# Turning the adapter activations in TensorE's transposing mode in a four-layer LoRA chain

## The chip, the cores and the metric

The kernel runs on one core of a Trainium2 chip. The metric is the device time of one execution in microseconds (us), as a median over several executions; lower is better. One more execution was recorded by the hardware profiler, and everything said of engines and waits below comes from that one.

## The reference, cut to what matters

Four residual layers are applied one after the other to `x` (8 batches of 256 tokens, 1024 features, fp32):

```python
x = x + L0(x)   # base weight quantized to a codebook, plus a LoRA of rank 64
x = x + L1(x)   # base weight, plus 8 experts of rank 16, top 2 by a softmax gate per token
x = x + L2(x)   # base weight and bias, plus the batch's own adapter of rank 16
x = x + L3(x)   # one of 16 weights, chosen by batch
```

The part that the change touches is in L2:

```python
lora_h = jnp.einsum('bti,bir->btr', x, A)         # 16 numbers per token: "h2"
lora_out = jnp.einsum('btr,bro->bto', lora_h, Bm)
return base_out + lora_out * SCALING
```

`lora_h` comes out of the kernel's products with tokens on the partitions, and the second product needs it with its rank on the partitions. So it has to be turned.

## The kernel before

**Phase 1** (about the first 230 us) multiplies the weights of L0, L1 and L2 into one another, so that the first three layers become a few wide products of `x`. Nearly every product is one of fp32 values, each split into a rounded high part and a remainder (type fp32r), in three matmuls: high by high, high by low, low by high (`product`, lines 992 to 994).

**Phase 2** runs over four groups `g` of 512 tokens (two batches each), three of them in a loop on every engine and the last written out. On TensorE a group is, in this order (`group`, written by hand):

- `x3_main(g, m)`: the m-th of eight blocks of 128 output features, 24 matmuls of 512 columns into bank `m % 5` of PSUM. `x3_main(g, 0)` comes first.
- `low_rank(g)`: for each of four tiles of 128 tokens, the expert activations, the gate's logits and h2, into banks 4 to 7 (lines 1079 and 1081). ScalarE and VectorE bring them to SBUF as `tok`; ScalarE then copies the h2 columns into `h2_tok`, 128 tokens by 32 columns per tile (16 for each batch, the other batch's columns zero), and VectorE works out the gates (`gating`) and scales the expert columns of `tok` by them.
- `x3_main(g, 1)`, `x3_main(g, 2)`.
- `turn_h2(g)` (lines 1116 to 1121): four matmuls with `h2_tok` as weights and the identity as moving operand put the turned h2 into partitions 0 to 31 of bank 5. `h2_tok` lies in the memory of `scales`, so the profile calls these `ps<-ident,scales`.
- `turn_g(g)` (lines 1123 to 1129): four 128 by 128 `pe.transpose` of the gated expert columns into bank 7. The profile calls these `ps<-ident,e_mid_w`.
- `x3_main(g, 3)`, then `h2_add(g)`, which adds onto bank 5 what the experts contribute to h2. It waits for `gt_done`: ScalarE (line 683) and VectorE (line 731) have brought bank 7 to SBUF.
- `x3_main(g, 4)`, then the gate and closing products of each block. `x3_close` needs the finished h2 (`h2_done`).
- `y_product(g, 0)` and `y_product(g, 1)`: L3, 192 matmuls of 512 columns each with weights streamed from HBM by SyncE's queue, split by ScalarE and VectorE into rings of four half tiles.

`turn_h2` raises no semaphore of its own. Its result is read after `h2_add`, whose last matmul raises `h2t_mm`.

Of the kernel before, what the change touches and what calls it, by code (L numbers as in the profile page):

```python
# [118 lines left out]
def build(nc, x, cb, lang, id2, id3, w0, scale_log, lora_a, lora_bt, w1, wrt, at, bcat,  # L119
          w2t, b, las, lbs, w3t, y):  # L120
    plan = phase1_plan()
    with ExitStack() as ctx:
# [866 lines left out]
        def _(pe):  # L989
# [126 lines left out]
            def turn_h2(g):  # L1116

                pe.wait_ge(h2_tok_done, 2 * (g + 1))
                for t in range(4):
                    pe.matmul(ps[0:32, 5, t * P:(t + 1) * P], h2_tok[:, t, :], ident[:, :],  # L1120
                              start=t == 0, stop=False, skip_group_check=True)

            def turn_g(g):

# [35 lines left out]
            def group(g):  # L1160
                x3_main(g, 0)
                low_rank(g)
                x3_main(g, 1)
                x3_main(g, 2)
                turn_h2(g)
                turn_g(g)
                x3_main(g, 3)
                h2_add(g)
                x3_main(g, 4)
                for m in range(3):  # L1170
                    x3_gate(g, m)
                pe.wait_ge(h2_done, g + 1)
                pe.wait_ge(bs_done, BS_CREDIT + 2 * (g + 1))
                for m in range(3):
                    x3_close(g, m)
                for m in range(3, 5):
                    x3_gate(g, m)
                    x3_close(g, m)
                for m in range(5, KT):
                    x3_main(g, m)  # L1180
                    x3_gate(g, m)
                    x3_close(g, m)
                y_product(g, 0)
                y_product(g, 1)
# [44 lines left out]
```

## Time and profile before

| | before |
|---|---|
| median of 3 runs | 678.62 us (678.43 to 678.86) |
| the profiled execution's own time | 679.95 us |
| its span (first to last instruction) | 678.1 us |
| TensorE matmuls, busy | 664.5 us, 98% of the span, 3280 instructions |
| TensorE weight loads, busy | 569.2 us, 84% |
| VectorE busy | 353.8 us, 52% |
| ScalarE busy | 279.3 us, 41% |
| GpSimd busy | 86.5 us, 13% |
| DMA | 67.59 MB, mean 100 GB/s |

A matmul of the program stands in the trace as a weight load (PEld) and a matmul (PE). Matmuls are pipelined: the duration of one, for example 273 ns, reaches over the start of the next, so what a matmul takes of TensorE's time is the distance from its start to the next one's start. The granted TensorE clock is given in tenths or as a number up to 1.00.

### The profile page before, as it was taken

To read this page: it belongs to the slowest core of one execution; us is meant where nothing else is said; L and a number is where in the kernel's file an instruction comes from. 1 tells how busy PE (TensorE), PEld (TensorE's weight loads), DVE (VectorE), ACT (ScalarE), POOL (GpSimd) and SP (SyncE) were. 2 spreads that over 40 slices of the span, in tenths; PEclk is the share of its full clock that TensorE was granted. 3 is DMA by queue.
4 is the path that set the end of the run, shared out by engine and by line. 5 is a ranking of instruction groups with operands and counts; after the bars stand their busy time and mean duration, and the time that the engine had idled before them with its cause. 6 is when DMAs were issued, how large, how long until landed. Compare 5 with 4: busy or idle time off the path is not lost.

```text
span 678.1 us, 9248 instructions
## 1 busy us (share of the span) xinstructions
PE 664.5 (98%) x3280; PEld 569.2 (84%) x3280; DVE 353.8 (52%) x535; ACT 279.3 (41%) x418; POOL 86.5 (13%) x122
## 2 busy tenths in 40 slices
PE   5998999999999999999999999999999999999998
PEld 5898999999999988888888788888788888888886
DVE  5689989879971384024543222661421653412453
ACT  5557483971912371124552122562121564121353
POOL 3210115004010030000120000221000221000120
PEclk9999999999999999999999999999999999999999
DMA  9661312001000504002774000677000586000362
GB/s 317 171 200 31 94 32 63 1 0 63 1 0 1 187 12 137 1 0 94 280 239 156 0 0 31 245 249 240 0 0 0 186 281 210 28 1 1 96 230 108
DMA packets 39330, 67.59 MB, mean 100 GB/s; under 512 B 3588, under 2 KB 23044, under 8 KB 39300
## 3 DMA queue, kind: packets, MB, share of 16 engines
q1 hardware_dynamic: 34448, 59.07, 26.7%
q10 hardware_dynamic: 4852, 8.13, 3.4%
q8 instruction: 18, 0.29, 0.2%
q14 instruction: 12, 0.10, 0.1%
HBM read 58.80 MB, written 8.39 MB: 99 GB/s over the span
## 4 chain that ended last, share of the span: by engine, by line
PE 92%; SPq 4%; DVE 2%; ACT 1%; issue 1%; DMA 0%; POOL 0%; ACTq 0%; DVEq 0%; POOLq 0%
PE ps L992 28%; PE ps L994 28%; PE ps L993 28%; PE ps L1079 3%; PE ps L1081 1%; SPq L342 1%; SPq L367 1%; PE ps L1112 1%; DVE tmp L802 1%; PE ps L1120 1%; SPq L366 1%; ACT tmp L547 0%; DMA e_both_w<-w_t 0%; SPq L337 0%; DVE w_w L792 0%
## 5 line engine op out<-in xcount | busy, mean ns | idle before, releaser
L992 PE MATMUL ps<-e_both,ring_hi 128*128 128x384 f32 (+3 forms) x384 | 134.6, 351 | 10.2 <-DVE e_both L731 8.3
L731 DVE TENSOR_TENSOR ring_lo<-raw,ring_hi 128x512 fp32r<-128x512 f32 x128 | 92.5, 736 | 80.9 <-ACT ring_hi L643 80.7
L994 PE MATMUL ps<-e_both,ring_lo 128*128 128x384 f32 (+3 forms) x384 | 134.1, 349 | 0.0
L643 ACT ACTIVATE ring_hi<-raw 128x512 fp32r<-128x512 f32 x128 | 79.4, 629 | 70.1 <-PE ps L994 65.9
L992 PE MATMUL ps<-x_both,e_both 128*128 128x512 f32 x256 | 101.5, 396 | 0.0
L993 PE MATMUL ps<-x_both,e_both 128*128 128x512 f32 x256 | 101.2, 395 | 0.0
L994 PE MATMUL ps<-x_both,e_both 128*128 128x512 f32 x256 | 101.0, 395 | 0.0
L992 PE MATMUL ps<-ring_hi,e_mid 128*128 128x512 f32 x256 | 101.0, 395 | 0.0
L994 PE MATMUL ps<-ring_hi,e_mid 128*128 128x512 f32 x256 | 101.0, 395 | 0.0
L993 PE MATMUL ps<-ring_lo,e_mid 128*128 128x512 f32 x256 | 101.0, 394 | 0.0
L992 PEld LDWEIGHTS ps<-e_both,ring_hi 128*128 128x128 f32 x384 | 72.8, 190 | 15.8 <-DVE e_both L731 8.3
L493 POOL TENSOR_TENSOR raw<-raw,ident 128x128 f32<-128x128 f32 x64 | 40.4, 633 | 320.2 <-DMA raw<-w_t 320.2
L994 PEld LDWEIGHTS ps<-e_both,ring_lo 128*128 128x128 f32 x384 | 72.7, 189 | 5.7
L966 DVE SCALAR_TENSOR_TENSOR e_mid<-ps,bias_col,e_mid 128x512 fp32r<-128x512 f32 x32 | 22.6, 746 | 94.7 <-ACT e_mid L689 94.7
L993 PE MATMUL ps<-e_mid,ring_hi 128*128 128x384 f32 (+2 forms) x192 | 68.5, 357 | 0.0
L993 PE MATMUL ps<-e_both,ring_hi 128*128 128x384 f32 (+2 forms) x192 | 65.5, 341 | 0.0
L547 ACT ACTIVATE tmp<-tmp,dif 128x1024 f32<-128x1024 f32 x48 | 54.1, 1150 | 21.3 <-DVE tmp L800 18.2
L802 DVE SCALAR_TENSOR_TENSOR tmp<-w_w,thr,tmp 128x1024 f32<-128x1024 f32 x48 | 60.4, 1302 | 4.4 <-ACT tmp L547 4.1
L689 ACT ACTIVATE e_mid<-ps,bias_col 128x512 fp32r<-128x512 f32 x32 | 20.4, 687 | 96.6 <-PE ps L1112 96.6
L993 PEld LDWEIGHTS ps<-ring_lo,e_mid 128*128 128x128 f32 x256 | 48.2, 188 | 11.3
L994 PEld LDWEIGHTS ps<-ring_hi,e_mid 128*128 128x128 f32 x256 | 48.2, 188 | 11.3
L994 PEld LDWEIGHTS ps<-x_both,e_both 128*128 128x128 f32 x256 | 48.1, 188 | 11.4
(144 smaller groups left out, 855.5 us busy)
## 6 DMA issues: line engine op xcount, KB each, us to landing
raw<-w_t SPq DMA_DIRECT2D x64, 512.0 KB, 3.6
xraw<-x_t SPq DMA_DIRECT2D x16, 512.0 KB, 4.8
w_w<-w SPq DMA_DIRECT2D x15, 512.0 KB, 5.1
y<-tmp ACTq DMA_DIRECT2D x30, 256.0 KB, 2.9
e_both_w<-w_t SPq DMA_DIRECT2D x4, 512.0 KB, 8.8
e_both_w<-w_t SPq DMA_DIRECT2D x4, 384.0 KB, 6.0
e_mid_w<-bs SPq DMA_DIRECT2D x24, 64.0 KB, 2.8
e_mid_w<-b_cat SPq DMA_DIRECT2D x1, 512.0 KB, 7.1
```

The source lines that it names most:

```text
L342: sp.dma_start(e_lo_w[:, ks, cols], w2t[2 * kk * P:2 * (kk + 1) * P, cols].rearrange("(k p) c -> p k c", p=P)).then_inc(s_w2[4 * c + kk], 16)
L493: pool.tensor_tensor(d, d, ident[:, :], ALU.add).then_inc(w3_diag, 1)
L547: act.activation(acc[i], acc[i], ACT.Identity, bias=dif[:, LEVELS - 1 - level:LEVELS - level]).then_inc(q_add, 1)
L643: act.activation(ring_hi[:, (2 * k + h) % 4, :], raw[:, k % RAW, h * 512:(h + 1) * 512], ACT.Copy).then_inc(w3_hi, 1)
L689: act.activation(x3_hi[:, m, :], ps[:, m % 5, :], ACT.Identity, bias=bias_col[:, m:m + 1]).then_inc(x3_hi_done, 1)
L731: return dve.tensor_tensor(out, whole, hi.bitcast(F32), ALU.subtract)
L802: ins = dve.scalar_tensor_tensor(out=acc[i], in0=qf, scalar=thr[:, k:k + 1], in1=acc[i], op0=ALU.is_gt, op1=ALU.mult)
L966: dve.scalar_tensor_tensor(out=x3_lo[:, m, :], in0=ps[:, m % 5, :], scalar=bias_col[:, m:m + 1], in1=x3_hi[:, m, :].bitcast(F32), op0=ALU.add,
L992: pe.matmul(out, a[0], b_[0], start=start, stop=False, **kw)
L993: pe.matmul(out, a[0], b_[1], start=False, stop=False, **kw)
L994: return pe.matmul(out, a[1], b_[0], start=False, stop=stop, **kw)
L1079: pe.matmul(ps[:, 4 + t, 0:2 * TW].rearrange("p (h c) -> p h c", h=2), x_hi[:, k, cols], e_both[:, :, k, ecols], start=k == 0, stop=False, ...
```

## The change

One keyword: the four matmuls of `turn_h2` are issued with `is_transpose=True`, as `pe.transpose` in `turn_g` issues its own. Operands, target, the `start` and `stop` flags, the wait and the place in the program stay.

```diff
@@ -1118,7 +1118,7 @@
                 pe.wait_ge(h2_tok_done, 2 * (g + 1))
                 for t in range(4):
                     pe.matmul(ps[0:32, 5, t * P:(t + 1) * P], h2_tok[:, t, :], ident[:, :],
-                              start=t == 0, stop=False, skip_group_check=True)
+                              start=t == 0, stop=False, is_transpose=True, skip_group_check=True)
 
             def turn_g(g):
 
```

## Rows read from the trace of the kernel before

**Rows 1.** The page: busy time and share of the span by engine.

```profile
PE 664.5 (98%) x3280; PEld 569.2 (84%) x3280; DVE 353.8 (52%) x535; ACT 279.3 (41%) x418; POOL 86.5 (13%) x122
```

**Rows 2.** Waits of engine PE, all: us in total, times, longest.

```profile
PE ps L992 <- DVE e_both L731: 8.3, 1, 8.3
PE ps L992 <- DVE ring_lo L731: 1.9, 1, 1.9
PE ps L1005 <- ACT raw L524: 0.2, 1, 0.2
```

**Rows 3.** Busy by stretch: length, busy us (count) per engine, PEclk, DMA share, GB/s.

```profile
0.00:17.00 17.00, 8.72 (x39) 8.71 (x40) 9.20 (x9) 10.02 (x12) 6.13 (x16) 1.00 0.94 316
55.00:271.00 216.00, 216.00 (x1175) 197.88 (x1174) 160.96 (x220) 109.47 (x148) 33.76 (x24) 1.00 0.15 49
271.00:378.00 107.00, 107.00 (x499) 87.92 (x499) 41.69 (x74) 36.73 (x61) 10.94 (x22) 1.00 0.35 122
...
592.00:678.10 86.10, 82.87 (x365) 66.58 (x363) 28.96 (x40) 27.70 (x45) 6.58 (x10) 1.00 0.25 86
```

**Rows 4.** Lines 1120 and 1128: form, count, duration ns min/median/max, first and last start.

```profile
L1120 PE MATMUL ps<-ident,scales x32: 272/273/297, 271.4 to 593.3; 128*32 128x128 f32 x32
L1128 PE MATMUL ps<-ident,e_mid_w x16: 272/273/329, 272.4 to 593.9; 128*128 128x128 f32 x16
```

**Rows 5.** Timeline of PE, group 0's turns: start us, us, what, xcount.

```profile
271.06 0.40 PE L994 MATMUL ps<-x_both,e_both 128*128 128x512 f32 x1
271.39 1.06 PE L1120 MATMUL ps<-ident,scales 128*32 128x128 f32 x8
272.38 0.66 PE L1128 MATMUL ps<-ident,e_mid_w 128*128 128x128 f32 x4
272.79 0.48 PE L992 MATMUL ps<-x_both,e_both 128*128 128x512 f32 x1
273.11 0.39 PE L993 MATMUL ps<-x_both,e_both 128*128 128x512 f32 x1
273.34 0.40 PE L994 MATMUL ps<-x_both,e_both 128*128 128x512 f32 x1
```

**Rows 6.** The same, windows that begin behind the first or only reach the last matmul.

```profile
271.52 0.93 PE L1120 MATMUL ps<-ident,scales 128*32 128x128 f32 x7
...
272.17 0.27 PE L1120 MATMUL ps<-ident,scales 128*32 128x128 f32 x1
...
272.54 0.49 PE L1128 MATMUL ps<-ident,e_mid_w 128*128 128x128 f32 x3
...
272.76 0.27 PE L1128 MATMUL ps<-ident,e_mid_w 128*128 128x128 f32 x1
```

**Rows 7.** Timeline of PE, group 3's turns.

```profile
592.54 1.06 PE L1120 MATMUL ps<-ident,scales 128*32 128x128 f32 x8
593.54 0.66 PE L1128 MATMUL ps<-ident,e_mid_w 128*128 128x128 f32 x4
593.95 0.48 PE L992 MATMUL ps<-x_both,e_both 128*128 128x512 f32 x1
```

**Rows 8.** Timeline of PE in group 0's `low_rank`: fp32r matmuls of 152 columns.

```profile
258.49 0.23 PE L1081 MATMUL ps<-e_both,x_both 128*128 128x152 f32 x1
258.56 0.35 PE L1079 MATMUL ps<-e_both,x_both 128*128 128x304 f32 x1
```

**Rows 9.** Timelines of DVE, ACT and PE: who feeds and who uses group 0's turns.

```profile
267.33 0.90 DVE L945 TENSOR_TENSOR e_mid_w<-e_mid_w,oh 128x128 f32<-128x128 f32 x4
...
273.70 0.69 DVE L731 TENSOR_TENSOR bc_lo<-ps,bc_hi 128x512 fp32r<-128x512 f32 x1 [4.16 <-ACT bc_hi L683]
...
261.81 0.35 ACT L674 ACTIVATE scales<-e_mid_w 128x32 f32<-128x32 f32 x2 [0.86 <-DVE e_mid_w L909]
...
278.47 0.28 PE L992 MATMUL ps<-bc_hi,br_now_hi 128*32 128x256 f32 x1
```

**Rows 10.** Timeline, end of the program.

```profile
674.47 0.40 PE L994 MATMUL ps<-ring_hi,e_mid 128*128 128x512 f32 x1
...
674.91 0.69 DVE L981 COPY tmp<-ps 128x512 f32<-128x512 f32 x1 [0.71 <-PE ps L994]
```

## The prediction

> **What bounds the kernel now.** The first view is the page's busy line [rows 1]: TensorE's matmuls fill 98% of the span, and the next engine, VectorE, 52%. Since matmuls overlap in the trace, this share alone doesn't say that TensorE sets the end, so the second view is the list of its waits [rows 2]: 10.4 us in three places and nothing else. The third view is the busy time by stretch [rows 3]. From 55 us to 592 us every stretch is as busy as it is long (216.00 of 216.00, 107.00 of 107.00; the two loop passes that aren't shown read the same), and in the last one 82.87 of 86.10 us are busy, the rest being the tail behind the last matmul. That matmul starts at 674.47 and one VectorE copy and its store follow it [rows 10]. So from 55 us on the time is TensorE's stream, matmul after matmul, with no wait for anybody, and a nanosecond taken out of the stream is a nanosecond off the end, as long as no wait opens that isn't there today.
>
> [...]
>
> **The turns now.** The count comes first [rows 4]. `turn_h2` has four matmuls per group and there are four groups, 16 in the program, yet line 1120 stands 32 times in the trace. `turn_g` also has 16, and line 1128 stands 16 times. So a plain fp32 matmul is issued as two passes, each with its weight load, and a transposing one as a single pass. Both kinds move 128 fp32 columns and both last 273 ns by themselves [rows 4]; what counts is how far apart they start. The second of the eight passes of line 1120 starts at 271.52 and the eighth at 272.17 [rows 6]: 0.65 us over six steps, 0.108 to 0.109 us each. On line 1128 the second starts at 272.54 and the fourth at 272.76 [rows 6]: 0.22 us over two steps, 0.11 us each. At equal moving width a transposing pass therefore takes the same 0.109 us of the stream as one of the two product passes, and I take 0.109 us for it.
>
> Is 0.109 us the moving side, or the weight load? The two lines differ in their weights, 32 columns against 128 [rows 4], and not in their step, so it isn't the weights. It isn't the issue of instructions either: a load and a matmul with 152 moving columns of fp32r give way to the next matmul after 0.07 us [rows 8]. So it goes by the moving fp32 columns, and these don't change.
>
> **The change, part by part.**
>
> Removed: in each group four of the eight passes of line 1120, 4 x 0.109 = 0.44 us. The whole stretch from the first pass of line 1120 to the first of line 1128 is now 272.38 - 271.39 = 0.99 us [rows 5], and in group 3 the same, 593.54 - 592.54 = 1.00 [rows 7]. It should become 0.99 - 0.44 = 0.55 us. Over four groups 4 x 0.437 = 1.75 us.
>
> Unchanged: the edges. In front of line 1120 a 512 column matmul starts at 271.06 and the first turn at 271.39, 0.33 us, where the step of such matmuls is 273.34 - 273.11 = 0.23: 0.10 us are lost [rows 5]. Between the last pass of line 1120 at 272.17 [rows 6] and line 1128 at 272.38 [rows 5] there are 0.21 us, 0.10 more than a step, and the first pass of line 1128 takes 272.54 - 272.38 = 0.16 us, 0.05 more than a step. Both kinds of edge sit where the waiting instruction is new, and the change leaves both waits. The trace doesn't show an edge between two transposing runs, so I bound it: the 0.15 us between the lines could vanish, which saves another 4 x 0.15 = 0.6 us, or as much could be added, which costs 0.6 us. I take zero, since the wait, which stays, is the nearest explanation of it.
>
> The one unknown price is that of a transposing pass whose weights have 32 columns, which the trace doesn't hold. From below: half a step, 0.055 us, were the mode to move columns at fp32r's rate (152 columns in 0.07 us [rows 8] make 0.059 us for 128). That would save 4 x 4 x (0.218 - 0.055) = 2.6 us. From above: no overlap at all, 0.273 us, the duration by itself [rows 4], which would cost 4 x 4 x (0.273 - 0.218) = 0.9 us more than today. I take 0.109 us, since line 1128 has the same mode, moving operand and type and differs only in the weights' width, which on line 1120 doesn't change the step.
>
> [...] Line 1128, at 0.109 us, is only twice as fast as two passes [rows 6], so the sum goes by the row.
>
> **What lies beside it and could open a wait.** Everything after `turn_h2` comes 0.44 us earlier per group relative to what isn't led by TensorE. The first to feel it is `turn_g`, which waits for the gated columns: VectorE's last write to them is done at 267.33 + 0.90 = 268.23, and `turn_g` starts at 272.38 [rows 5, 9]. It has 4.1 us in hand and needs 0.44. `turn_h2`'s own input is ready at 262.16 [rows 9]. Next is `h2_add` at 278.47, which waits for ScalarE and VectorE to bring `turn_g`'s result over. They finish at 273.70 + 0.69 = 274.39 [rows 9], 4.1 us ahead, and they start off `turn_g`, so they move with it. No other engine gets or loses an instruction, and SyncE's and GpSimd's queues stay as they are. The later waits of TensorE (split weights, split `x`) cost nothing in any group [rows 2], and their refills are released by TensorE itself.
>
> **Sum.** In the profiled execution the span goes from 678.1 to 676.35 us, and its time from 679.95, 1.85 above the span, to 678.2. That execution is 1.3 us above the median of the runs, so for the median 678.62 - 1.75 = **676.9 us**, 0.26% faster. What a measurement of this kernel can tell from no change is 0.2%, 1.36 us, so the bound lies at 677.26 and the forecast clears it by only 0.4 us.
>
> **Rivals.**
>
> *The mode gives nothing at this width (the change doesn't do what it says).* The weights have 32 columns and the output takes 32 partitions, where line 1128 has 128 of both. If a narrow turn is issued in two passes after all, the stream is the same and the time 678.6 us. If it is one pass but the turns don't overlap (0.273 us each), it is 4 x 0.22 = 0.9 us longer, 679.5 us. For it: no row shows this form. Against it: the narrow plain pass overlaps its neighbours as well as the wide one does [rows 6]. [...] Chance 0.09.
>
> *The clock falls.* This is the case that ends slower. Today transposing passes alone hold TensorE for 0.41 us (272.38 to 272.79 [rows 5]) and the clock stays at 1.00 [rows 3]; with the change they hold it for 0.55 + 0.41 = 0.96 us in one piece. [...] It decides only if the stretch of about 1 us is already enough to lower the clock. Against it stands the start of the program: there TensorE is busy for 8.72 of 17 us and is granted 1.00 [rows 3]. [...] Chance 0.02.
>
> *The gain is swallowed by a wait.* The only candidates are `turn_g`, `h2_add` and the split weights, and the first two have 4.1 us in hand. It would give about 678.6 us. Chance 0.02.
>
> *The mode is twice as fast again* (0.055 us per turn): 678.62 - 2.6 = 676.0 us. Chance 0.04. Line 1128 speaks against it.
>
> **How the numbers follow.** The forecast has 0.83, the rest is as above. Its own spread is the edge, 0.6 us either way around 676.9, and about 0.1 us for the median, so 676.2 to 677.6 us. This holds over 8 in 10, and the range needn't reach to the rivals. Faster by over 0.2%: most of the forecast's 0.83 (0.04 of it may end above 677.26, if an edge grows) and the 0.04 of the faster mode, 0.83 in all. Within 0.2%: 0.04 from the forecast, 0.07 of the first rival, 0.02 of the swallowed gain, 0.13. Slower by over 0.2%: the clock, 0.02, and 0.02 of the first rival, for turns that are slower still than 0.273 us.
>
> **What would show it.** In the profile of the changed kernel line 1120 stands 16 times in place of 32, and PE has 3264 instructions in place of 3280. The four start 0.109 us apart. From line 1120's first start to line 1128's there are 0.55 us in each group, and from one group's turns to the next 106.6 us in place of 107.05. The clock stays at 1.00 in the stretch behind the turns, and the list of TensorE's waits gets no new line. It is wrong if line 1120 still stands 32 times or the 0.99 us remain (first rival), if the clock is under 1.00 around the turns (second), or if the turns shrink and the next start on line 1120 is still 107.05 us on (third). If the four start 0.055 us apart, the size was wrong and not the mechanism.

## The result and the profile after

| | before | after |
|---|---|---|
| median, first comparison | 678.67 us (6 runs) | 675.36 us (674.58 to 675.95, 6 runs) |
| ratio, 95% interval | | 0.9952 [0.9941, 0.9962] |
| median, second comparison | 678.37 us (21 runs) | 675.48 us (675.09 to 675.95, 5 runs) |
| ratio, 95% interval | | 0.9958 [0.9945, 0.9972] |
| span of the profiled execution | 678.1 us | 673.8 us |
| granted clock | 1.00 | 1.00 |

The change makes the kernel faster, by 3.3 us in the first comparison (2.6 to 4.0 by its interval) and 2.9 us in the second. The forecast was 1.75 us, 676.9 us with a range from 676.2 to 677.6, so the direction was right and the time lies below the range.

The page of the changed kernel, busy time by engine (before: [rows 1]):

```profile
PE 661.4 (98%) x3264; PEld 567.8 (84%) x3264; DVE 354.1 (53%) x535; ACT 279.6 (41%) x418; POOL 89.0 (13%) x122
```

There are 16 matmuls and 16 weight loads fewer, as forecast, and nothing else has another count. Lines 1120 and 1128 by form (count, duration ns min/median/max, first and last start; before: [rows 4]):

```profile
L1120 PE MATMUL ps<-ident,scales x16: 270/272/273, 269.9 to 589.1; 128*32 128x128 f32 x16
L1128 PE MATMUL ps<-ident,e_mid_w x16: 272/273/273, 270.3 to 589.6; 128*128 128x128 f32 x16
```

So the mode halves the passes of a turn with 32 weight columns too. The largest durations say something more: before, they were 297 and 329 ns [rows 4], in the first pass of each line; now the largest is 273 ns and no pass stands out. The timeline of TensorE around group 0's turns (start us, us, what, count; before: [rows 5]):

```profile
269.40 0.40 PE L993 MATMUL ps<-x_both,e_both 128*128 128x512 f32 x1
269.64 0.39 PE L994 MATMUL ps<-x_both,e_both 128*128 128x512 f32 x1
269.87 0.60 PE L1120 MATMUL ps<-ident,scales 128*32 128x128 f32 x4
270.30 0.60 PE L1128 MATMUL ps<-ident,e_mid_w 128*128 128x128 f32 x4
270.66 0.48 PE L992 MATMUL ps<-x_both,e_both 128*128 128x512 f32 x1
```

From line 1120's start to line 1128's there are 0.43 us. That is four steps of 0.109 us and nothing else; I had expected 0.55. In front of line 1120 there are 0.23 us, the plain step of a matmul of 512 columns, where there had been 0.33 [rows 5]. And `turn_g` takes 0.36 us to the next block, where it took 0.41 [rows 5]. From the matmul ahead of the turns to the block behind them it was 272.79 - 271.06 = 1.73 us [rows 5] and is 270.66 - 269.64 = 1.02, so 0.71 us less per group, 2.8 us over four. Of these 0.44 per group are the removed passes and **0.27 are losses at the edges of line 1120**, which the forecast had left standing.

The weight loads (engine PEld) show what these losses are in the trace. The first weight load of line 1120, before:

```profile
271.38 0.79 PEld L1120 LDWEIGHTS ps<-ident,scales 128*32 128x32 f32 x8 [0.37 <-issue]
```

and in the changed kernel:

```profile
269.64 0.54 PEld L1120 LDWEIGHTS ps<-ident,scales 128*32 128x32 f32 x4
```

Before, the loading side sits idle for 0.37 us, in which it waits for no other engine that the profile shows (`issue`), and the load starts only when its own matmul does, at 271.39 [rows 5]. After, it starts with the matmul ahead of the turns, at 269.64, and is out of the way when the first turn starts at 269.87. The same holds for the first load of line 1128: 272.38, together with its matmul, before, and 270.20, 0.10 us ahead of it, after.

The span fell by 4.3 us, 1.5 more than that. Group 0's turns start at 269.87 where they started at 271.39 [rows 5], and only 0.10 of this difference is the entry. The waits of TensorE, all of them (us in total, times, longest; before: [rows 2]):

```profile
PE ps L992 <- DVE e_both L731: 8.0, 1, 8.0
PE ps L992 <- DVE ring_lo L731: 0.8, 1, 0.8
PE ps L1005 <- ACT raw L524: 0.2, 1, 0.2
```

They are in phase 1, which the change doesn't touch, and are 1.4 us shorter in sum. In the profiled executions of the nine kernels below, which are the same in phase 1, the sum of these waits is between 7.8 and 9.5 us, also where the turns are plain fp32, and the profiled execution of before (10.4 us) was itself 1.3 us above the median of its runs. So this part is the spread from one execution to the next and no effect of the change. The list has no new line, and the clock is 1.00 behind the turns too (length, busy us by engine, clock, DMA share, GB/s):

```profile
270.65:276.30 5.65, 5.65 (x27) 4.53 (x26) 0.69 (x1) 0.60 (x1) 0.00 (x0) 1.00 0.01 3
```

### The profile page after: what moved, and what is told of

Read it like the earlier page. It is cut to its first block, busy times and chain, and to the rows that moved or that the text cites. A ratio compares the mean times of both kernels' runs of the same rounds, so it can differ in the third digit from the quotient of the medians.

```text
span 673.8 us, 9216 instructions
## 1 busy us (share of the span) xinstructions
PE 661.4 (98%) x3264; PEld 567.8 (84%) x3264; DVE 354.1 (53%) x535; ACT 279.6 (41%) x418; POOL 89.0 (13%) x122
## 4 chain that ended last, share of the span: by engine, by line
PE 92%; SPq 4%; DVE 2%; ACT 1%; issue 1%; DMA 0%; POOL 0%; ACTq 0%; DVEq 0%; POOLq 0%
PE ps L992 28%; PE ps L993 28%; PE ps L994 28%; PE ps L1079 3%; PE ps L1081 1%; SPq L342 1%; SPq L367 1%; PE ps L1112 1%; ACT tmp L547 1%; SPq L366 1%; SPq L337 0%; DMA e_both_w<-w_t 0%; DVE w_w L798 0%; DVE tmp L802 0%; DVE w_w L792 0%
```

## The experiments

Where did the 0.27 us at the edges come from? Three theories were set against one another. **A**: it is lost where a matmul that drives only a part of the array's columns (32 weight columns) meets matmuls that drive all of it. **B**: it is lost where a plain fp32 matmul in two passes meets another kind. **C**: it goes with the wait on a semaphore in front of the turns, which was my reading in the prediction. The rows below are TensorE's timeline around group 0's turns, with the columns start us, us, what, count. The other three groups of each run have the same steps to 0.003 us.

### The changed kernel once more

> The changed kernel once more, for its size. Removed passes alone (4 x 4 x 0.109 us) make 1.75 us, 676.9 us. The first profile also shows the losses in front of and behind line 1120 gone (0.27 us per group, 1.08 in all), which makes 2.83 us and 675.85 us. If there is a third gain outside the turns, the median stays at 675.4 us or below. Between line 1120's first start and line 1128's first start I expect 0.43 us in every group, and from group to group 106.35 us.

Measured: 675.48 us, ratio 0.9958 [0.9945, 0.9972], which on 678.37 us is 2.85 us, with 1.9 to 3.7 by the interval. The same 16 passes and steps as in the first profile. The sum of 0.71 us four times, 2.8, lies in both intervals; the 1.75 of the forecast lies in neither. The expectation's 675.85 us was reckoned from the first comparison's 678.67; from this one's 678.37 it is 675.5, which is what was measured, so no third gain is needed. From group to group it is 106.31 us in both profiles of the changed kernel, against 107.05 before: 0.74 us, of which 0.03 us lie in the matmuls behind the turns and stay unexplained (0.1 us over four groups).

The removed passes and the edges together are the size. Theory C is already hard to hold: the waits in front of lines 1120 and 1128 are still there, and their losses aren't.

### Plain fp32, full width

The weights of each turn are widened from 32 to 128 columns.

```diff
+        h2_pad = sb("h2_pad", [P, 7 * 32], F32)
...
-        h2_tok = scales[:, :, :, :].rearrange("p a k e -> p (a k e)").rearrange("p (t c) -> p t c", t=4)
+        h2_tok = h2_pad[:, 0:P].rearrange("p (t c) -> p t c", t=4)
...
-            pool.memset(h2_tok[:, :, :], 0.0).then_inc(h2_clear, 1)
+            pool.memset(h2_pad[:, :], 0.0).then_inc(h2_clear, 1)
...
-                    pe.matmul(ps[0:32, 5, t * P:(t + 1) * P], h2_tok[:, t, :], ident[:, :],
+                    pe.matmul(ps[:, 5, t * P:(t + 1) * P], h2_pad[:, 32 * t:32 * t + P], ident[:, :],
                               start=t == 0, stop=False, skip_group_check=True)
```

> Plain fp32 in two passes as before, but the weights padded with zeros to 128 columns, so that each turn fills the whole array and writes 128 partitions; the result in partitions 0 to 31 is the same. Theory A (the loss comes where a matmul on 32 columns of the array meets matmuls on all of it): the loss is gone with the two passes still there; line 1120 stands 32 times, 0.87 us from its first start to line 1128's instead of 0.99, 0.23 us in front of it instead of 0.33, 0.27 us less per group, time 678.67 - 1.08 = 677.6 us. Theory B (the loss comes where a plain fp32 matmul meets one of another kind, whatever its width): 0.99 and 0.33 us stay, time 678.7 us.

Measured: 677.64 us (11 runs), ratio 0.9989 [0.9980, 0.9998]. The timeline (lines 1123 and 1131 are `turn_h2` and `turn_g` here, and the trace calls the padded tile `h_pad`):

```profile
270.03 0.40 PE L997 MATMUL ps<-x_both,e_both 128*128 128x512 f32 x1
270.27 1.05 PE L1123 MATMUL ps<-ident,h_pad 128*128 128x128 f32 x8
271.16 0.60 PE L1131 MATMUL ps<-ident,e_mid_w 128*128 128x128 f32 x4
271.51 0.48 PE L995 MATMUL ps<-x_both,e_both 128*128 128x512 f32 x1
```

All eight passes are still there, and the losses are gone: 0.24 us in front, 0.89 us for eight passes (0.111 each), 0.35 for `turn_g`. Four times as many weight columns, the same number of passes, and less time. That is theory A's outcome, and B is refuted: a plain fp32 matmul meets the others without loss if it is 128 columns wide. From the matmul ahead to the block behind it is 1.48 us against 1.73 [rows 5], 0.25 less per group and 1.0 over four. The medians moved by 0.7 us, the interval (0.1 to 1.4 us) holds both, and the starts carry the verdict. The weight load is ahead again as well, 0.23 us before the first pass at 270.27:

```profile
270.04 1.09 PEld L1123 LDWEIGHTS ps<-ident,h_pad 128*128 128x128 f32 x8
```

Two things about the edit. The added columns aren't all zeros, as the expectation has it: the weights of turn `t` are columns `32 * t` to `32 * t + 127` of `h2_pad`, and its first 128 columns hold all four tiles, so turn 0 takes the other three tiles along and only turn 3 has 96 zero columns. What they produce lands in partitions 32 to 127 of the bank, which nobody reads. And the weights also moved to another tile. The run with 64 columns below has the same tile and the whole loss, so it isn't the place in memory.

### Transposing mode, full width

The same padding on the changed kernel, `is_transpose=True` kept.

> The changed kernel with the same padding to 128 columns. Theories A and B both: four turns 0.109 us apart, no loss at either side, the same time as the changed kernel, 675.4 to 675.9 us. If the width of the weights cost anything, more than that.

Measured: 675.80 us (675.35 to 675.83), ratio 0.9960 [0.9947, 0.9974].

```profile
269.72 0.39 PE L997 MATMUL ps<-x_both,e_both 128*128 128x512 f32 x1
269.95 0.60 PE L1123 MATMUL ps<-ident,h_pad 128*128 128x128 f32 x4
270.38 0.60 PE L1131 MATMUL ps<-ident,e_mid_w 128*128 128x128 f32 x4
270.74 0.48 PE L995 MATMUL ps<-x_both,e_both 128*128 128x512 f32 x1
```

Each step is that of the changed kernel to 0.01 us. In transposing mode 32 columns and 128 behave alike. With the run before it this also separates the two parts: at full width the mode is worth the four removed passes only (0.89 against 0.43 us).

### Two visits, plain and transposing

```diff
-            def turn_h2(g):
+            def turn_h2(g, part):
...
-                for t in range(4):
+                for t in (2 * part, 2 * part + 1):
...
+                turn_h2(g, 0)
                 x3_main(g, 2)
-                turn_h2(g)
+                turn_h2(g, 1)
                 turn_g(g)
```

`turn_h2(g, part)` issues the turns of tiles 0 and 1, or of 2 and 3. Plain fp32, 32 columns:

> Plain fp32 as before, but two of the four turns of a group are issued ahead of the third block of 24 matmuls and two behind it: the same eight passes in two visits. If the loss is paid at each visit's entry and exit (A and B both), it doubles: 0.33 us in front of both visits, and about 0.17 to 0.27 us more per group, 679.4 to 679.8 us. If it was the wait on a semaphore in front of the first turn and in front of line 1128 that cost (theory C), there is no wait in front of the new entry at the second visit and only the first entry shows 0.33 us; time 678.7 us.

Measured: 679.83 us (11 runs), ratio 1.0021 [1.0012, 1.0030], slower than before by 1.4 us (0.8 to 2.0). The first of group 0's two visits:

```profile
264.22 0.40 PE L994 MATMUL ps<-x_both,e_both 128*128 128x512 f32 x1
264.55 0.62 PE L1120 MATMUL ps<-ident,scales 128*32 128x128 f32 x4
265.10 0.50 PE L992 MATMUL ps<-x_both,e_both 128*128 128x512 f32 x1
265.44 0.39 PE L993 MATMUL ps<-x_both,e_both 128*128 128x512 f32 x1
```

and the second:

```profile
270.55 0.40 PE L994 MATMUL ps<-x_both,e_both 128*128 128x512 f32 x1
270.88 0.62 PE L1120 MATMUL ps<-ident,scales 128*32 128x128 f32 x4
271.43 0.65 PE L1128 MATMUL ps<-ident,e_mid_w 128*128 128x128 f32 x4
271.84 0.48 PE L992 MATMUL ps<-x_both,e_both 128*128 128x512 f32 x1
```

Both visits pay 0.33 us in front, and four passes take 0.55 us where four steps are 0.44. From line 994 at 264.22 to line 993 at 265.44 it is 1.22 us, of which 0.44 are passes and 2 x 0.23 the steps of the two large matmuls: about 0.32 are lost at this visit, and it comes on top of the old one: at the second visit, from 270.55 to 271.84, 0.27 are lost as before. The expectation had 0.17 to 0.27 us for the added visit, a little too little. Four times 0.32 are 1.3 us, within the measured 0.8 to 2.0. The loss goes by visits and not by passes. For theory C the expectation erred: the second visit issues the same wait as the first, so its entry tells nothing. The next run does, since it has the same waits at the same places.

Transposing, the same two visits:

> The changed kernel with its four transposing turns in two visits, two ahead of the third block of 24 matmuls and two behind it, as the plain turns in the run with two visits. Theory A (the loss belongs to matmuls that drive a part of the array, and the transposing turns drive all of it): a second visit is free, 0.23 us in front of both visits, 0.109 us steps, the same time as the changed kernel, 675.4 to 675.9 us. If the transposing mode only hides the loss because line 1128 follows in the same mode, the first visit, which fp32r matmuls follow, shows an exit of 0.2 us and the time is about 676.3 us.

Measured: 675.60 us (674.86 to 676.40), ratio 0.9959 [0.9945, 0.9972], the same as the changed kernel.

```profile
263.27 0.39 PE L994 MATMUL ps<-x_both,e_both 128*128 128x512 f32 x1
263.50 0.38 PE L1120 MATMUL ps<-ident,scales 128*32 128x128 f32 x2
263.64 0.48 PE L992 MATMUL ps<-x_both,e_both 128*128 128x512 f32 x1
263.95 0.39 PE L993 MATMUL ps<-x_both,e_both 128*128 128x512 f32 x1
```

From line 994 at 263.27 to line 993 at 263.95 it is 0.68 us, and the two steps of 0.23 and the two turns of 0.11 are 0.68 too. (Line 992 starts 0.03 us behind the last turn and its own step is 0.32 us, and behind `turn_g` it is 0.03 and 0.31 to 0.32 in every profile; only the sum counts.) There is no loss, with fp32r matmuls on both sides, so the mode doesn't need a neighbour in the same mode. The waits are those of the plain run with two visits, which lost 0.32 us here: theory C is refuted.

### Something else that is narrow

One more matmul per group goes between the two runs of turns of the changed kernel, into bank 7, which `turn_g` overwrites. First bf16, 32 columns:

```diff
+                pe.matmul(ps[0:32, 7, 0:P], ident[:, :].bitcast(mybir.dt.bfloat16)[:, 0:32],
+                          ident[:, :].bitcast(mybir.dt.bfloat16)[:, 0:P], start=True, stop=True,
+                          skip_group_check=True)
```

> The changed kernel with one more matmul per group between the two runs of turns: bf16, 32 weight columns, 128 moving columns, into partitions 0 to 31 of bank 7, which line 1128 then overwrites. It is one pass and not fp32. Theory A (narrow against full array): the loss comes back around it, about 0.1 us in front of it and 0.1 to 0.16 us behind it, so that from the last pass of line 1120 to the second of line 1128 there are 0.43 to 0.5 us instead of the 0.27 to 0.28 us without a loss. Theory B (plain two-pass fp32 against other kinds): no loss, 0.27 to 0.28 us. In time 1.0 us or less in all, which one look doesn't resolve; the starts do.

Measured in one run: 676.47 us. (This run and the three that follow are single ones, for their starts; one run of before beside them took 678.81 us.) (`turn_g` is line 1131 in this kernel and the next.)

```profile
269.41 0.60 PE L1120 MATMUL ps<-ident,scales 128*32 128x128 f32 x4
269.94 0.23 PE L1122 MATMUL ps<-ident 128*32 128x128 bf16 x1
270.10 0.66 PE L1131 MATMUL ps<-ident,e_mid_w 128*128 128x128 f32 x4
270.51 0.48 PE L992 MATMUL ps<-x_both,e_both 128*128 128x512 f32 x1
```

Then the same with 128 columns, as a control:

> The same with 128 weight columns and all 128 partitions, as a control. Theories A and B both: no loss, the bf16 matmul takes 0.055 to 0.11 us and line 1128's passes are 0.109 us apart from the first on. If a loss shows here, it comes with a change of the number type and neither theory holds.

Measured in one run: 675.67 us.

```profile
269.58 0.60 PE L1120 MATMUL ps<-ident,scales 128*32 128x128 f32 x4
270.02 0.22 PE L1122 MATMUL ps<-ident 128*128 128x128 bf16 x1
270.07 0.61 PE L1131 MATMUL ps<-ident,e_mid_w 128*128 128x128 f32 x4
270.44 0.48 PE L992 MATMUL ps<-x_both,e_both 128*128 128x512 f32 x1
```

The two differ in the width alone. From line 1120's start to the block behind the turns it is 1.10 us with 32 columns and 0.86 with 128: the narrow one costs 0.24 us more, though it loads a quarter of the weights. The four turns in front of it last 0.53 us instead of 0.44, the matmul itself holds 0.16 us instead of 0.05, and `turn_g` is 0.41 long again instead of 0.37. From the last pass of line 1120 to the second of line 1131 the narrow one takes 0.20 + 0.16 + 0.17 = 0.53 us, a little over the expected 0.43 to 0.5, and the wide one 0.11 + 0.05 + 0.12 = 0.28. So the loss that theory A forecast comes for a matmul that is neither fp32 nor in two passes.

One plain fp32 matmul with 32 columns in the same place:

> The changed kernel with one plain fp32 matmul (two passes, 32 weight columns) between the two runs of turns. Theories A and B both: the entry and the exit loss come back in full though only one narrow matmul is left: 0.2 us from the last transposing turn to its first pass, 0.2 us from its second pass to line 1128, line 1128's first step 0.166 us. If the loss grew with the number of narrow passes, it would be a quarter of that.

Measured in one run: 677.10 us. (`turn_g` is line 1130.)

```profile
269.31 0.60 PE L1120 MATMUL ps<-ident,scales 128*32 128x128 f32 x4
269.84 0.41 PE L1122 MATMUL ps<-ident,scales 128*32 128x128 f32 x2
270.18 0.65 PE L1130 MATMUL ps<-ident,e_mid_w 128*128 128x128 f32 x4
270.59 0.48 PE L992 MATMUL ps<-x_both,e_both 128*128 128x512 f32 x1
```

1.28 us where the changed kernel has 0.79: 0.22 are its two passes and 0.27 the edges, the full price for a single matmul.

### Plain fp32, 64 columns

The full-width plain kernel with `ps[0:64, ...]` and `h2_pad[:, 32 * t:32 * t + 64]`.

> The plain fp32 turns of before with weights padded to 64 columns instead of 32 or 128. Theory A in the form that any use of a part of the array costs: entry 0.33 us and exit 0.20 us as with 32 columns, 107.05 us from group to group. If only the narrowest use costs, or if the loss falls with the width, 0.23 us and 0.11 us as with 128 columns and 106.8 us from group to group, or something between.

Measured in one run: 678.50 us.

```profile
269.50 0.40 PE L997 MATMUL ps<-x_both,e_both 128*128 128x512 f32 x1
269.83 1.09 PE L1123 MATMUL ps<-ident,h_pad 128*64 128x128 f32 x8
270.85 0.66 PE L1131 MATMUL ps<-ident,e_mid_w 128*128 128x128 f32 x4
271.26 0.48 PE L995 MATMUL ps<-x_both,e_both 128*128 128x512 f32 x1
```

0.33 in front, 1.02 to `turn_g`, 0.41 for `turn_g`, 1.76 in all against 1.73 with 32 columns [rows 5]: the loss is whole at half the width, 0.03 us larger even. The 0.03 us are in the first own step (0.16 us against 0.13), not at the entry, which is 0.33 us as with 32 columns. It didn't fade from 32 to 64 columns; of the three widths tried, only 128 is free of it.

## Why the prediction was wrong in size

**What bounds the kernel: right.** TensorE's stream set the end, and what was taken out of it came off the time: 0.71 us per group in the starts, 2.8 over four, 2.85 us in the second comparison's ratio. From group to group it is 106.31 us where 106.6 were forecast.

**Passes and step: right.** 16 fewer passes, the new form's step 0.109 us, taken from line 1128. The 0.43 us for four turns are 0.109 each, a factor of two against the two passes of 0.109. So the rival with turns twice as fast again, 0.055 us each and 676.0 us, is refuted too, though its time lies nearer to the measured one than the forecast's.

**The edges: this is the step that failed.** The prediction measured them, 0.10 us in front, 0.10 between the lines and 0.05 in `turn_g`'s first pass [rows 5, 6], and then took their change to be zero, "since the wait, which stays, is the nearest explanation of it". With the first step of line 1120 (0.13 us, 0.02 more than a step [rows 5, 6]) they make 0.27 us per group, and all of it went. The waits stayed. The full-width plain run shows what the loss belongs to: with passes, waits and place in the program unchanged and the width at 128 it was gone. The bound was short as well: it gave the vanishing of the 0.15 us between the lines, 0.6 us, and left out the 0.10 in front and 0.02 in the first step, which have the same cause. With all of them the term is 4 x 0.27 = 1.1 us and the forecast 675.8 us, 0.4 above the median of the first comparison and 0.3 above that of the second.

The profile before would have spoken against the wait as cause, in two ways. `h2_add` is behind a wait too, and is entered one plain step of 0.23 us behind the matmul ahead of it, with its weight load ahead (before):

```profile
278.24 0.40 PE L994 MATMUL ps<-x_both,e_both 128*128 128x512 f32 x1
278.24 0.11 PEld L992 LDWEIGHTS ps<-bc_hi,br_now_hi 128*32 128x32 f32 x1
278.47 0.28 PE L992 MATMUL ps<-bc_hi,br_now_hi 128*32 128x256 f32 x1
```

And what `turn_h2` and `turn_g` wait for had been there for 9.2 and 4.1 us [rows 5, 9].

`h2_add` has 32 weight columns as well and shows no loss at either side (0.23 us in front, and 0.11 from its last matmul at 279.06 to the next block at 279.17, where its steps are 0.12), which narrows theory A: plain fp32 with 32 or 64 columns (0.27 and 0.30 us a visit) and bf16 with 32 (0.24) lose, fp32r and the transposing mode with 32 don't. So the runs show for which of the forms tried the loss comes, and that the weight load at such a crossing starts only with its own matmul (271.38 and 271.39). Why these forms differ they don't show.

**The first rival, no gain at this width: refuted.** With 32 weight columns a transposing turn is one pass (line 1120 stands 16 times), its step is 0.109 us and not 0.273, and it has no loss at the edges; the 32 and 128 column turns are alike to 0.01 us. That the transposing turns, and the fp32r products of `h2_add`, drive the whole array would fit this and is my guess from the alike steps; no run shows it, as the trace doesn't tell which columns a matmul drives.

**The clock: refuted.** 1.00 behind 0.79 us of transposing passes in one piece (269.87 to 270.66), and the mean granted clock of every execution, of all kernels, is 0.999 or 1.000.

**The swallowed gain: refuted.** No new wait.

**What stays open.** How far the first comparison's 3.3 us is more than 2.85: its interval reaches from 2.6, so nothing has to be explained, and phase 1's waits differ by 1.4 us between two executions. Why the first step with 64 columns costs 0.03 us more than with 32 wasn't tried, nor was any width between 64 and 128. The number of weight columns and that of the output partitions always changed together, so which of the two counts isn't shown. Why the weight load of a narrow plain fp32 or bf16 matmul doesn't get ahead is open.

## What to carry to other kernels

In a stream that TensorE alone bounds, count what a stretch takes from start to start, edges included, and not passes times step: here more than a third of what could be had (0.27 of 0.71 us) lay at the edges. The weight loads of the trace show such an edge at a glance: the load started with its own matmul (271.38 and 271.39) and not with the one ahead (269.64, 0.23 us before its own). Where a few plain fp32 matmuls with 32 or 64 weight columns, or a bf16 one with 32, stand between full ones, widening the weights to 128 columns is worth trying, if the other partitions of the bank are free: for the fp32 turns it cost 0.002 us a pass here and took away 0.27 us per visit, 0.24 for the bf16 matmul. Or gather the small ones into one visit: a second one cost 0.32 us. A pure turn of fp32 did best in the transposing mode, which had half the passes (0.43 us for four turns against 0.99 with 32 columns) and none of this loss.

## What was not expected of the hardware

- A plain fp32 matmul with 32 or 64 weight columns between matmuls with 128 cost about 0.1 us at its entry, 0.1 us at its exit, and 0.02 to 0.06 us each in the first step of either run: with 32 columns 0.27 us for a visit of eight passes and for a visit of two, 0.32 for a visit of four with fp32r matmuls behind it, with 64 columns 0.30 for eight. One bf16 matmul with 32 columns cost 0.24 us more than with 128.
- At such a crossing the weight load started within 0.01 us of its own matmul (271.38 and 271.39), where without the loss it started 0.23 us ahead (269.64 and 269.87).
- The loss went by the visit and not by the number of passes, and was 0 at 128 columns, where eight passes took 0.89 us against 0.99 with 32 columns.
- fp32r matmuls (`h2_add`, entered 0.23 us behind the matmul ahead) and transposing fp32 matmuls (steps of 0.109 us, entry 0.23) with 32 weight columns showed none of it.
